# Attention with a gated output: out preloaded with x and accumulated into by DMA, the gate multiply on VectorE, row tiles and waits moved

## The reference

```python
xn = layernorm(x)                       # over the 4096 columns, no scale
q = xn @ Wq.T + bq                      # 32 heads of 128
k = xn @ Wk.T + bk                      # 16 heads
v = xn @ Wv.T + bv                      # 16 heads
w = softmax(causal(q @ k.T / sqrt(32))) # query heads h and h+16 share a k/v head
s = w @ v
logits = xn @ router_W.T                # 8 experts, the best two kept, renormalized
mid = (xn @ lora_A) * w_dense           # rank 16 per expert
g = silu(xn @ base_W.T + 2 * (mid @ lora_B))
out = x + s * g
```

## Time and profile before

| what | us |
|---|---|
| median of 2 runs | 2538.75 |
| the two runs | 2392.04 and 2685.47 |
| the profiled execution | 2395.89 |
| its span, slowest core | 2394.0 |
| spans of its eight cores | 2372.7 to 2394.0 |
| busy: TensorE, ScalarE, VectorE, GpSimd | 1826.1, 553.2, 332.6, 233.2 |

### The profile page before, as it was taken

The page is one execution under the profiler, slowest core; times in us unless marked ns, Lnnn a source line. Parts: engine busy times, 40 slices in busy tenths (PEclk is TensorE's granted clock), DMA queues, the critical chain, the costliest instruction groups (busy, mean ns, idle before and its releaser), DMA issues.

```text
span 2394.0 us, 33894 instructions; the slowest of 8 cores (2372.7 to 2394.0 us)
## 1 busy us (share of the span) xinstructions
PE 1826.1 (76%) x13156; PEld 1160.3 (48%) x13156; DVE 332.6 (14%) x1043; ACT 553.2 (23%) x677; POOL 233.2 (10%) x124
## 2 busy tenths in 40 slices
PE   5520599999999998399995999999975362754770
PEld 1100244444444445288873888888852141432440
DVE  0169100000000000400000000000015152322220
ACT  5500001101101100111100111111124372855880
POOL 1100000000000000000000000000000606014006
PEclk9955799999999998699998999999987696987995
DMA  9700455444445455123105244333123535234115
GB/s 153 130 0 0 44 59 64 56 55 56 55 59 67 56 72 72 24 46 50 30 17 74 57 80 79 75 74 71 39 56 97 196 79 216 64 124 147 41 31 209
DMA packets 232845, 177.97 MB, mean 74 GB/s; under 512 B 123763, under 2 KB 219124, under 8 KB 226420
## 3 DMA queue, kind: packets, MB, share of 16 engines
q0 software_dynamic: 155408, 85.53, 26.1%
q1 hardware_dynamic: 72676, 56.73, 7.9%
q10 hardware_dynamic: 4608, 33.56, 3.9%
HBM read 194.20 MB, written 50.33 MB: 102 GB/s over the span
## 4 chain that ended last, share of the span: by engine, by line
PE 64%; DMA 11%; ACT 8%; DVE 8%; issue 4%; POOL 4%; SPq 0%; DVEq 0%; ACTq 0%; POOLq 0%
PE pg L333 28%; PE pg L526 19%; PE pg L431 9%; ACT arena L705 7%; DMA arena<-xT 4%; DMA arena<-gH 2%; DMA arena<-Qs 2%; POOL arena L745 2%; POOL arena L749 2%; DVE arena L718 2%; DVE arena L295 2%; DVE arena L292 2%; PE pav L600 2%; PE pg L492 1%; PE psA L698 1%
## 5 line engine op out<-in xcount | busy, mean ns | idle before, releaser
L333 PE MATMUL pg<-arena,wstr 128*128 128x512 bf16 x3072 | 665.8, 380 | 104.9 <-DMA wstr<-wqT 104.9
L333 PEld LDWEIGHTS pg<-arena,wstr 128*128 128x128 bf16 x3072 | 301.2, 98 | 470.7 <-issue 110.0
L526 PE MATMUL pg<-wstr,arena 128*128 128x256 bf16 x4096 | 463.0, 273 | 24.6 <-DMA wstr<-bwT 24.6
L526 PEld LDWEIGHTS pg<-wstr,arena 128*128 128x128 bf16 x4096 | 401.6, 98 | 72.4 <-issue 25.1
L431 PE MATMUL pg<-wstr,arena 128*128 128x256 bf16 x2048 | 239.9, 276 | 40.5 <-ACT vsb L442 40.5
L431 PEld LDWEIGHTS pg<-wstr,arena 128*128 128x128 bf16 x2048 | 197.7, 99 | 72.5 <-issue 40.6
L698 PE MATMUL psA<-arena 128*128 128x512 bf16 x320 | 103.5, 407 | 168.0 <-ACT arena L705 122.4
L705 ACT ACTIVATE arena<-psA,konst 128x1024 bf16<-128x1024 f32 x160 | 178.4, 1115 | 143.8 <-DMA out<-arena 102.3
L705 ACT ACTIVATE arena<-psB,konst 128x1024 bf16<-128x1024 f32 x160 | 178.5, 1115 | 67.4 <-PE psB L698 65.0
L342 ACT ACTIVATE vsb<-pg,bq_sb 128x512 bf16<-128x512 f32 x64 | 44.1, 689 | 541.9 <-PE pg L333 541.9
L538 ACT ACTIVATE vsb<-pg 128x256 f32<-128x256 f32 x128 | 49.3, 385 | 407.3 <-PE pg L532 407.3
(11 more groups left out here) (82 smaller groups left out, 802.1 us busy)
## 6 DMA issues: line engine op xcount, KB each, us to landing
arena<-xT POOLq DMA_DIRECT2D x32, 512.0 KB, 12.0
wstr<-wqT POOLq DMA_DIRECT2D x16, 1024.0 KB, 12.6
wstr<-bwT POOLq DMA_DIRECT2D x8, 2048.0 KB, 16.7
gH<-vsb SPq DMA_DIRECT2D x128, 128.0 KB, 1.9
arena<-xsel ACTq DMA_DIRECT2D x16, 1024.0 KB, 6.3
arena<-gH ACTq DMA_DIRECT2D x16, 1024.0 KB, 8.8
out<-arena POOLq DMA_DIRECT2D x16, 1024.0 KB, 4.3
Qs<-vsb SPq DMA_DIRECT2D x64, 128.0 KB, 2.1
```

What stands on the lines that cost most here:

```text
L333: em.emit("T", lambda E, pp=pp, sl=sl, ch=ch, ts=ts: nc.tensor.matmul(pp[:, :], wbuf[sl][:, ch * 128:(ch + 1) * 128], xnT[:, ch * T + ts * ...
L526: em.emit("T", lambda E, pp=pp, sl=sl, ch=ch, tc=tc: nc.tensor.matmul(pp[:, 0:256], xnT[:, ch * T + tc * 128: ch * T + tc * 128 + 128], bw ...
```

## The change

Into phase A's start four DRAM to DRAM copies on SP's queue put x into `out`. At a block's end, x is no longer loaded and added: the multiply by g moves to VectorE, and GpSimd's store adds the piece to what is in `out` (`accum_op`). g has four slots and is loaded inside the block, at units 4, 7, 10 and 13. The quotients of a block wait for the stores of the block before instead of for its add. In phases A and B `mrow` and `qrow` move to the second half of `wstr`, `rrow` to `vsb`, the first two weight loads lose their waits for `anrm` and `asq`, and the first 32 products wait for `anrm` one chunk at a time.

```diff
-        x_slot = [arena32[:, 8192:10240], arena32[:, 10240:12288]]
-        g_slot = [arena32[:, 12288:14336], arena32[:, 14336:16384]]
+        g_slot = [arena32[:, 8192 + 2048 * i: 8192 + 2048 * (i + 1)]
+                  for i in range(4)]
...
-        mrow = wstr32[0:1, 0:2048]
-        qrow = wstr32[0:1, 2048:4096]
-        rrow = wstr32[0:1, 4096:6144]
+        mrow = wstr32[0:1, 4096:6144]
+        qrow = wstr32[0:1, 6144:8192]
...
+        rrow = vsb32[0:1, 0:2048]
...
+        for i in range(4):
+            em.emit("Y", lambda E, i=i: E.dma_start(
+                out[i * 512:(i + 1) * 512, :], xsel[i * 512:(i + 1) * 512, :]),
+                inc=("dpre", 16))
...
-                w = ([("anrm", ANRM), ("asq", em.c("asq"))] if og < 2
-                     else [("bwu%d" % sl, og // 2)])
+                w = [] if og < 2 else [("bwu%d" % sl, og // 2)]
...
-                    if og < 2 and ts == 0:
-                        w.append(("anrm", ANRM))
                     for ch in range(NCH):
...
+                        wch = w if ch == 0 else []
+                        if og == 0 and ts == 0:
+                            wch = list(wch) + [("anrm", 2 * (ch + 1))]
...
-            def emit_xg(qs, qc):
-                sl = qc % 2
+            def emit_g(qs, qc):
                 w = []
-                if xg_use[sl] > 0:
-                    w.append(("dof%d" % sl, 16 * xg_use[sl]))
-                elif qs == 0:
+                if qs > 0:
+                    w.append(("dfin", 4 * (qs - 1) + qc + 1))
+                elif qs == 0 and qc < 2:
                     w += G_ST
...
-                em.emit("S", lambda E, sl=sl, r0=r0: E.dma_start(
-                    x_slot[sl][:, :], xsel[r0:r0 + 128, :]),
-                    waits=w, inc=("dxg%d" % sl, 16))
-                em.emit("S", lambda E, sl=sl, r0=r0: E.dma_start(
-                    g_slot[sl][:, :], gH[r0:r0 + 128, :]),
-                    inc=("dxg%d" % sl, 16))
-                xg_cnt[(qs, qc)] = em.c("dxg%d" % sl)
+                em.emit("S", lambda E, qc=qc, r0=r0: E.dma_start(
+                    g_slot[qc][:, :], gH[r0:r0 + 128, :]),
+                    waits=w, inc=("dg%d" % qc, 16))
...
                         waits=[("dvc", em.c("dvc")),
-                               ("dfin", 4 * (qs - 1) + qc + 1 if qs > 0 else 0)],
+                               ("dofq%d" % qc, 16 * qs)],
                         inc=("f_" + pname, 1))
...
+                        if u in (4, 7, 10, 13):
+                            emit_g(qs, (u - 4) // 3)
...
                 for qc in range(4):
-                    emit_xg(qs, qc)
-                    sl = qc % 2
                     r0 = qs * 512 + qc * 128
-                    w = SEV + [("dxg%d" % sl, xg_cnt[(qs, qc)]),
-                               ("dfc", em.c("dfc")), ("dfin", em.c("dfin"))]
-                    em.emit("P", lambda E, sl=sl, qc=qc: nc.gpsimd.tensor_mul(
+                    w = SEV + [("dg%d" % qc, 16 * (qs + 1)),
+                               ("dofq%d" % qc, 16 * qs),
+                               ("dfin", em.c("dfin"))]
+                    em.emit("V", lambda E, qc=qc: nc.vector.tensor_mul(
                         s_sb[:, qc * 2048:(qc + 1) * 2048],
-                        s_sb[:, qc * 2048:(qc + 1) * 2048], g_slot[sl][:, :]),
-                        waits=w, inc=("dfc", 1))
-                    em.emit("P", lambda E, sl=sl, qc=qc: nc.gpsimd.tensor_add(
-                        x_slot[sl][:, :], x_slot[sl][:, :],
-                        s_sb[:, qc * 2048:(qc + 1) * 2048]),
-                        waits=[("dfc", em.c("dfc"))], inc=("dfin", 1))
-                    em.emit("P", lambda E, sl=sl, r0=r0: E.dma_start(
-                        out[r0:r0 + 128, :], x_slot[sl][:, :]),
-                        waits=[("dfin", em.c("dfin"))], inc=("dof%d" % sl, 16))
+                        s_sb[:, qc * 2048:(qc + 1) * 2048], g_slot[qc][:, :]),
+                        waits=w, inc=("dfin", 1))
+                    em.emit("P", lambda E, qc=qc, r0=r0: E.dma_start(
+                        out[r0:r0 + 128, :], s_sb[:, qc * 2048:(qc + 1) * 2048],
+                        accum_op=ALU.add),
+                        waits=[("dfin", em.c("dfin")), ("dpre", 64)],
+                        inc=("dofq%d" % qc, 16))
```

More of the change, by code:

```diff
@@ L336, in build_program @@
                             start=(ch == 0), stop=(ch == NCH - 1)),
-                            waits=w if ch == 0 else (),
+                            waits=wch,
                             inc=grp_inc)
@@ L558, in build_program @@
             vsr = Vs.rearrange("(kc p) (h d) -> p kc h d", p=128, d=128)
-            xg_cnt = {}
-            def emit_xg(qs, qc):
-                sl = qc % 2
+            def emit_g(qs, qc):
                 w = []
-                if xg_use[sl] > 0:
-                    w.append(("dof%d" % sl, 16 * xg_use[sl]))
-                elif qs == 0:
+                if qs > 0:
+                    w.append(("dfin", 4 * (qs - 1) + qc + 1))
+                elif qs == 0 and qc < 2:
                     w += G_ST
-                xg_use[sl] += 1
                 r0 = qs * 512 + qc * 128
-                em.emit("S", lambda E, sl=sl, r0=r0: E.dma_start(
-                    x_slot[sl][:, :], xsel[r0:r0 + 128, :]),
-                    waits=w, inc=("dxg%d" % sl, 16))
-                em.emit("S", lambda E, sl=sl, r0=r0: E.dma_start(
-                    g_slot[sl][:, :], gH[r0:r0 + 128, :]),
-                    inc=("dxg%d" % sl, 16))
-                xg_cnt[(qs, qc)] = em.c("dxg%d" % sl)
+                em.emit("S", lambda E, qc=qc, r0=r0: E.dma_start(
+                    g_slot[qc][:, :], gH[r0:r0 + 128, :]),
+                    waits=w, inc=("dg%d" % qc, 16))
             avbanks = [(pav[0], "pav0"), (pav[1], "pav1"), (pg[0], "pg0"), (pg[1], "pg1")]
@@ L739, in build_program @@
                 for qc in range(4):
-                    emit_xg(qs, qc)
-                    sl = qc % 2
                     r0 = qs * 512 + qc * 128
-                    w = SEV + [("dxg%d" % sl, xg_cnt[(qs, qc)]),
-                               ("dfc", em.c("dfc")), ("dfin", em.c("dfin"))]
-                    em.emit("P", lambda E, sl=sl, qc=qc: nc.gpsimd.tensor_mul(
+                    w = SEV + [("dg%d" % qc, 16 * (qs + 1)),
+                               ("dofq%d" % qc, 16 * qs),
+                               ("dfin", em.c("dfin"))]
+                    em.emit("V", lambda E, qc=qc: nc.vector.tensor_mul(
                         s_sb[:, qc * 2048:(qc + 1) * 2048],
-                        s_sb[:, qc * 2048:(qc + 1) * 2048], g_slot[sl][:, :]),
-                        waits=w, inc=("dfc", 1))
-                    em.emit("P", lambda E, sl=sl, qc=qc: nc.gpsimd.tensor_add(
-                        x_slot[sl][:, :], x_slot[sl][:, :],
-                        s_sb[:, qc * 2048:(qc + 1) * 2048]),
-                        waits=[("dfc", em.c("dfc"))], inc=("dfin", 1))
-                    em.emit("P", lambda E, sl=sl, r0=r0: E.dma_start(
-                        out[r0:r0 + 128, :], x_slot[sl][:, :]),
-                        waits=[("dfin", em.c("dfin"))], inc=("dof%d" % sl, 16))
+                        s_sb[:, qc * 2048:(qc + 1) * 2048], g_slot[qc][:, :]),
[5 more added lines that the diff above has]
+                        inc=("dofq%d" % qc, 16))
                     out_ct += 1
             em.emit("Y", lambda E: E.nop(),
-                    waits=[("dof0", 16 * xg_use[0]), ("dof1", 16 * xg_use[1])])
+                    waits=[("dofq%d" % qc, 64) for qc in range(4)])
         with nc.Block() as block:
```

## The result

The changed kernel is slower by 1.1%: ratio 1.0114, 95% interval 1.009 to 1.0139, which is clear of no change though under 2%. Its median is 2423.0 us of 9 runs beside 2397.9 us of 8 runs of the kernel before; some executions of either kernel are disturbed and up to 12% longer, and the ratio leaves them out. The profiled execution took 2426.8 us with a span of 2424.9, on core 2. The forecast was 2378 us, 0.7% less than before; the time came out inside the range, which was 170 us wide, and on the other side of no change.

What follows compares the result with a forecast made beforehand. Bounds: full DMA engines during xT loads, VectorE alone until 249 us, matrix products, then attention block ends waiting on stores. 2395.9 - 83 (block ends) - 28 (tail) + 8 (g loads) + 85 (copies) = 2378 us; range 2295 to 2465.

Steps and rivals of the forecast that it cites:

- the block ends: End of attention query blocks 0 to 2: 49 us lost instead of 132, a gain of 83 us.
- the copies: Phase A, x to out beside the xT loads: 85 us added, bounded by 41 (lower still, 0) and 99.
- the tail: From the last quotient to the end: 27 us instead of 54.6, a gain of 28 us.
- the band with the chance of 0.45: Whole kernel: the forecast with the hidden-weight-load case, a time between 2348 and 2444 us, chance 0.45.
- the accumulating store: Stores of out at block ends: 5.5 us per MB, first landing 7.2 us after issue, last 26.2 after the last quotient.
- the twelve later loads of g: Attention after block 0: twelve issues, 5.4 us, taken as hidden beside exponentials, so 0 us.
- Rivals 2 and 3: Phase A copies: 2, engine price of 41 us, 2334 us, chance 0.15; 3, hidden in idle window, 2293 us, 0.05.
- The loads of g in block 0: Attention block 0, where TensorE already waits for Q: four loads at 2 us each, 8 us added.
- Phases A and B otherwise: Weakened waits and moved rows: 0 us, since the barrier stays; the 17.8 us to the first product not hidden.
- Rival 5: Phases A to B: the change does hide the weight load, 18 us less, 2360 us; chance within the forecast's 0.45.
- Rival 1: Block ends and tail: accumulating store costs what a plain one does, gains 110 and 40, 2339 us; chance 0.13.
- Rival 4: Block ends: slow accumulating store, VectorE waits in ScalarE's place; 2466 us at 11 us per MB; chance 0.22.

## Why the prediction was wrong

The signs of the mechanisms were right, and the sum had the wrong sign because three terms were mis-sized, all against the change. It forecast -18 us (-83 - 28 + 8 + 85) and the profiled executions differ by +31, 49 us apart: 32 at the block ends, 16 in the copies, 5 in the tail, less 4 that the loads of g and the rest cost under their 8. With the copies alone put right the forecast would still have been 2394, 2 us under before; the block ends are the larger step. That the time fell inside the range, and inside the band with the chance of 0.45, is owed to their width.

The block ends: 83 us gain forecast, 51 measured. Of the missing 32 us, 17 are the accumulating store, and its price is the step that failed. It was put at 5.5 us per MB and a first landing 7.2 us after the issue; at the end of block 0 the first quotient was released 9.8 us after the first issue, the tail shows 6.5 us per MB, and the fourth landing came 31.5, 33.5 and 32.2 us after the last quotient at the three block ends in place of 26.2, 5 to 7 us more each time. Against plain stores the accumulation costs 44 us there, where the forecast had 49 - 22 = 27. The Trainium skill (Collectives: The Full Stack, section The bandwidth ceiling) has the add of a reduction read two sources for each piece written, which I had turned into an estimate of 5.9 us. The 6.5 us, 2.5 times the plain store's engine time, are more than that rule's doubling; the reads themselves no run shows.

Another 10 us were lost away from the block ends, in the middle of block 1. Here the step that failed is a term of nothing: the forecast put the twelve later loads of g at nothing, because their issues are hidden behind exponentials; it left out that their data runs beside the loads of Q. In before these units take 5.0 to 5.5 us, in the changed kernel 6.8 to 8.7. The loads of V for the next block stand there too, in both kernels, and no run takes the loads of g out alone, so their share stays open.

The last 5 are the rest of the block ends: with plain stores they lose 27 us where I had 22, a figure for which the prediction shows no working. VectorE's four products took 9.48 us for the 9.3 of the forecast, and TensorE does wait for the masks behind them, 7.1 us in the kernel with both kinds of buffers.

What the account of a block end left out as well are the loads of Q, which are issued behind the accumulating stores and take up to 14.7 us there. They hardly added to the miss, since the wait for the landed stores runs beside them; but the runs with one result buffer or two, and two Q buffers or six, show that this wait alone holds the block end about as long as the one I had counted.

The copies: 85 us forecast, 101 measured. The step that failed is the choice of 85 below the upper bound of 99, which I had worked out from all bytes in memory, 33.6 MB at 340 GB/s. The bound was the answer: 163 to 175 GB/s written while copies run, in long pieces, short pieces or alone. The rule of the Trainium skill (HBM Reference, section Specifications (TRN2)) that I weighed against it, about 358 GB/s per core with both cores of a pair streaming, gave 89 us. The 326 to 350 GB/s of DRAM traffic in these runs lie 2 to 9% below it, for reads alone and for reads and writes together. Rivals 2 and 3 fall with it: the 41 us were the price of a store, which has only one side in DRAM, and the xT loads weren't served first but last. That most of the copy's time passed before xT moved at all I hadn't foreseen; the run in short pieces shows that it made no difference to when phase A was done.

The tail: 28 us gain forecast, 23 measured, with the plain store 38 (54.6 to 16.5) for my 40. The step that was off is again the accumulating store.

The loads of g in block 0 were put at 8 us. All that came between the first weight load and the end of block 0 is 3.8 us, 1.7 of them ahead of the first product, so about 2 can be theirs.

Phases A and B otherwise: 0 forecast, 1.7 us measured. The first product came 19.5 us after the first weight load was issued, with the barrier where it was (17.8 before). Rival 5, as a reading of the edit, is confirmed the other way about: with the barrier taken out, the same waits and the same row tiles give 26 us.

Rival 1 (the accumulating store costs what a plain one does) is refuted by 16.2 against 4.8 us to landing. Rival 4 was the nearest in kind: VectorE does take ScalarE's place at the block ends. But 6.5 us per MB is far from its threshold of 9.6, and phase A grew by 101, under the 110 that would have been a sign: neither sign of being wrong was met. It took several smaller misses on the same side.

## What to carry to other kernels

Before a transfer is moved to where "nothing needs it", look at the DMA share of that stretch and count the bytes on both sides: a copy within DRAM costs its bytes twice, and at share 1.0 all of it is added to what runs there. The same copy in a stretch with share 0 cost nothing here and turned +1.1% into -3.4%.
An accumulating store replaced a load and an add by a store that took 2.5 times the engine time of a plain one. What waits for its buffer, and every small load issued behind it, then needs a buffer more; each edit alone can show no gain while both together do. Before buffers are added for one kind of load, see what else stands in front of it in its queue: here a load of K with two buffers held those of Q with six.
A wait that is weakened gains nothing while a barrier stands in front of it: compare the lists of instructions, not the waits.

## What was not expected of the hardware

With 64 KB pieces in one queue and 8 KB rows in the other, the loads of xT went down from one every 3 us to one every 27 to 47 us; with 4 KB pieces they went on at one every 5 to 7 us. The two streams together were done within 5 us of the same time.

Reads and writes of DRAM by one core's DMAs, with all eight cores at it, summed to 326 to 350 GB/s in each mixture (two times 163, one times 340, two times 175), while copies within SBUF ran at 406 GB/s in either direction at once.

A load of 128 KB, with a median of 2.7 us to landing, took 14.7 us behind 4 MB of accumulating stores from another queue.
